# A kernel of two attentions and two expert mixtures: new written-out orders of all engines and new PSUM banks

## What is computed

```python
x = x + _L0_xattn_ref(_layernorm(x), ctx_768, Wq, Wk, Wv, Wo, bo)       # 8 heads of 64
x = x + _L0_ffn_ref(_layernorm(x), w_gate, w1_e, w3_e, w2_e, w1_s, w3_s, w2_s)
x = x + _L1_xattn_ref(_layernorm(x), ctx_768, Wq, Wk, Wv, Wo)           # 16 heads of 8
x = x + _L1_ffn_ref(_layernorm(x), router_w, experts_bias, w1, w3, w2, sw1, sw3, sw2)

# _L0_ffn_ref: 16 experts of 64, sigmoid scores, 2 of 4 groups, 4 experts
scores = jax.nn.sigmoid(x @ w_gate.T)
w = w / (w.sum(-1, keepdims=True) + 1e-06) * ROUTE_SCALE
routed = jnp.einsum('tef,ehf,te->th', silu(x w1_e) * (x w3_e), w2_e, combine)
return (routed + shared).reshape(shape)

# _L1_ffn_ref: 8 experts of 256, the 2 of the highest logits
logits = xf @ router_w.T + experts_bias
rw, sel = jax.lax.top_k(logits, K)
rw = jax.nn.softmax(rw)
moe_out = jnp.einsum('te,teh,ehd->td', cw, silu(g) * u, w2)
```

## Time and profile before

| | us |
|---|---|
| median of 3 runs | 230.97 |
| profiled execution, device time | 231.44 |
| its span | 229.6 |
| PE busy in the span | 223.2 |
| DVE busy | 164.1 |
| ACT busy | 152.8 |
| POOL busy | 126.4 |

### The profile page before, as it was taken

The page is one execution under the profiler, slowest core; times in us unless marked ns, Lnnn a source line. Parts: engine busy times, 40 slices in busy tenths (PEclk is TensorE's granted clock), DMA queues, the critical chain, the costliest instruction groups (busy, mean ns, idle before and its releaser), DMA issues.

```text
span 229.6 us, 4315 instructions
## 1 busy us (share of the span) xinstructions
PE 223.2 (97%) x1389; PEld 166.7 (73%) x1389; DVE 164.1 (71%) x482; ACT 152.8 (67%) x376; POOL 126.4 (55%) x127
## 2 busy tenths in 40 slices
PE   7999999999999999999999999999999999999994
PEld 3576765965889898889535563588878888888883
DVE  3689984788667963699948983564867785776874
ACT  2579999986679445672689778876464554645561
POOL 2866742899046927857492107208499500996540
PEclk9999999999999999999999999999999999999999
DMA  6790000000029925900600000027000003700002
GB/s 207 202 302 7 0 3 0 0 3 1 3 80 238 370 105 148 218 3 4 217 3 3 3 1 6 0 67 305 0 0 0 3 0 97 274 0 4 0 0 91
DMA packets 10172, 17.04 MB, mean 74 GB/s; under 512 B 3715, under 2 KB 5540, under 8 KB 9766
## 3 DMA queue, kind: packets, MB, share of 16 engines
q1 hardware_dynamic: 9926, 16.45, 23.0%
q10 hardware_dynamic: 224, 0.32, 0.4%
HBM read 16.08 MB, written 0.62 MB: 73 GB/s over the span
## 4 chain that ended last, share of the span: by engine, by line
PE 86%; ACT 6%; DVE 4%; POOL 2%; issue 1%; DVEq 0%; POOLq 0%
PE psum L1181 12%; PE psum L1185 11%; PE psum L1182 11%; PE psum L1354 7%; ACT prob L749 5%; PE psum L1416 5%; PE psum L1362 4%; PE psum L1364 3%; PE psum L1363 3%; PE psum L1472 3%; PE psum L1300 3%; PE psum L1312 3%; PE psum L1437 2%; PE psum L1276 2%; PE psum L1189 2%; PE psum L1460 2%
## 5 line engine op out<-in xcount | busy, mean ns | idle before, releaser
L703 POOL TENSOR_TENSOR act_s<-act_s,spread 128x512 f32<-128x512 f32 x35 | 44.3, 1289 | 20.2 <-DMA spread<-cw 14.1
L1181 PE MATMUL psum<-xT_hi,w_hi 128*128 128x512 f32 x108 | 43.9, 406 | 0.0
L1185 PE MATMUL psum<-xT_lo,w_hi 128*128 128x512 f32 x108 | 42.3, 391 | 0.0
L1182 PE MATMUL psum<-xT_hi,w_lo 128*128 128x512 f32 x108 | 42.1, 390 | 0.0
L798 ACT CAST q<-psum 128x512 fp32r<-128x512 f32 x35 | 20.4, 587 | 21.4 <-PE psum L1364 15.1
L1009 DVE TENSOR_TENSOR q<-psum,q 128x512 fp32r<-128x512 f32 x35 | 23.8, 687 | 13.5 <-ACT q L798 13.0
L788 ACT ACTIVATE act_s<-psum 128x512 f32<-128x512 f32 x39 | 23.1, 597 | 12.3 <-PE psum L1185 7.9
L1152 DVE TENSOR_REDUCE neg_max<-psum 128x2 f32<-128x308 f32 x64 | 26.2, 472 | 4.6 <-PE psum L1416 4.4
L703 POOL TENSOR_TENSOR hid<-hid,spread 128x512 f32<-128x512 f32 x13 | 16.5, 1286 | 18.7 <-DMA spread<-cw 14.4
L652 POOL TENSOR_TENSOR rstd<-vareps,minus_half 128x4 f32<-128x4 f32 x8 | 8.1, 1018 | 33.4 <-DVE vareps L910 33.4
L646 POOL TENSOR_TENSOR w_lo<-w_src,w_hi 128x768 fp32r<-128x768 f32 x12 | 21.8, 1835 | 8.6 <-ACT w_hi L718 8.6
(11 more groups left out here) (173 smaller groups left out, 467.0 us busy)
## 6 DMA issues: line engine op xcount, KB each, us to landing
spread<-cw SPq DMA_DIRECT2D x16, 256.0 KB, 4.6
spread<-cw SPq DMA_DIRECT2D x6, 512.0 KB, 5.6
w_src<-in_w SPq DMA_DIRECT2D x2, 1152.0 KB, 5.1
w_src<-in_w SPq DMA_DIRECT2D x1, 2304.0 KB, 10.9
spread<-cw SPq DMA_DIRECT2D x8, 128.0 KB, 2.9
w<-in_w SPq DMA_DIRECT2D x1, 576.0 KB, 6.6
out<-X SPq DMA_DIRECT2D x4, 128.0 KB, 1.8
wv<-in_wv SPq DMA_DIRECT2D x2, 192.0 KB, 4.8
```

The source lines that it names most:

```text
L703: pool.tensor_tensor(g, g, spread[:, slot, :], ALU.mult).then_inc(weighed, 1)
L1181: pe.matmul(dst, w_hi, xT_hi[:, b, :], start=True, stop=False)
L1182: pe.matmul(dst, w_lo, xT_hi[:, b, :], start=False, stop=False)
L1185: return pe.matmul(dst, w_hi, xT_lo[:, b, :], start=False, stop=True)
```

## The change

The table `PROGRAM` gets new strings for all five engines, and new banks for PE's steps. The steps are the same; what a step computes doesn't change. In the new order on PE, among others: the first xT goes ahead of three of the four kT; xT(1,0) goes ahead of the third k1 and of two pT steps; one scores step goes ahead of the first wo. On ACT, 21 `score` steps stand ahead of the fourth pT copy of batch 0, where there were 19; six `place_k1` go behind the first q1 copies of batch 0; three splits of `w2_1` go behind the last exponentials. On SP, `fetch w13_1` goes ahead of the fifth spread, and `fetch w2_1` one place_max later.

With the orders come waits that no longer lean on them. `need` (new) remembers for each engine and semaphore the highest count waited for and issues a wait only when it asks for more; `wait_filled` and `wait_moved` go through it. Waits that one step made for all that followed it on its engine are now asked by each step (`loaded`, `lo_of`, `xT_rounded`). DVE's `res` no longer waits for its own read; the lnA of sublayer 2 does.

```diff
@@ -150,68 +150,68 @@
 
 PROGRAM = {
     "PE":
-        "kT.0 kT.1 kT.0 kT.2 xT.3 vf.1 vf1.4 q.2 q.3 q.4 xT.2 q.3 scores.4.0 scores.3.1 scores.2.5 scores.6.7 " +
-        "scores.0.4 vf.3 q.1 q.2 scores.3.5 scores.6.1 vs.7 pT.2 scores.7.0 pT.4 q.3 pT.2 q.5 pT.6 scores.1.4 " +
-        "pT.7 pT.5 pT.2 k1.6 pT.0 scores.1.7 pT.2 pT.0 pT.5 pT.2 scores.6.4 rest.2.0.1.3 scores.7.5 pv pv pv " +
-        "pv scores.7.0 scores.1.2 scores.3.4 pT.6 wo.5 pT.0 pT.6 wo.1 scores.0.5 pT.3 pT.2 k1.4 vf1.6 vs1.0 " +
-        "pT.5 pT.3 pT.1 pT.2 k1.7 xT.6 k1.2 pT.4 pT.1 pT.6 gate.3 rest.1.6.4.5 pv pv pv pv h1.4 h1.6 wo.5 " +
-        "wo.1 cwT.3 h1.4 h1.3 h3.1 h3.4 h1.7 h3.1 xT.3 h3.0 h1.6 h3.5 gate.3 h3.7 h3.2 down.4 down down h1.1 " +
-        "h1.6 h1.0 h3.1 h3.5 h3.0 down h1.6 down down down down cwT.3 h3.1 down h1.0 h3.3 h1.4 h1.0 h3.5 h1.4 " +
-        "h1.6 xT.2 down.7 h3.4 h1.0 qd.2 down down q1.2.6.3.1 down score1.2 score1.5 h3.0 score1.2 score1.3 " +
-        "score1.6 score1.1 score1.5 h1.4 score1.3 score1.2 h1.6 down score1.5 score1.1 score1.3 score1.0 h3.4 " +
-        "score1.6 score1.1 score1.5 score1.2 down h3.4 h3.6 mT.5 down score1.5 score1.4 down score1.5 " +
-        "score1.4 score1.6 down expT.4.5 score1.6 score1.2 expT.1.0 expR.7 expR.3 score1.4 score1.5 score1.6 " +
-        "score1.2 expT.4.1 score1.5 xT.6 score1.2 score1.7 rest1.3.5 score1.0 qd.6 mT.0 expT.1.7 pv1 " +
...
+        "kT.7 xT.6 kT.5 kT.4 kT.3 q.2 q.4 q.6 q.5 xT.7 scores.2.6 vf1.3 scores.1.4 scores.0.5 scores.2.7 q.6 q.1 " +
+        "vf1.4 vs.3 scores.0.6 scores.5.1 scores.2.4 pT.7 pT.3 q.0 pT.7 q.6 scores.5.7 scores.3.1 pT.0 pT.2 k1.4 pT.6 " +
+        "vf.5 scores.7.0 scores.6.2 pT.3 pT.1 pT.5 pT.7 pT.4 pT.0 vf.5 rest.3.6.1.0 scores.7.4 pv pv pv pv scores.5.2 " +
+        "scores.6.1 scores.4.0 scores.7.3 wo.5 pT.2 pT.6 pT.1 wo.5 k1.0 pT.6 pT.2 vs1.7 pT.1 pT.4 xT.3 pT.6 pT.2 k1.0 " +
+        "h1.4 gate.3 pT.7 pT.0 pT.2 h3.6 rest.5.1.7.2 k1.0 pv pv pv pv wo.1 cwT.3 wo.2 h1.7 h1.5 h3.2 h3.4 h1.1 h1.3 " +
+        "h1.6 xT.7 down.5 h3.3 h1.1 h3.6 h3.2 gate.7 h1.4 down h1.3 down h3.1 down down down h1.3 h3.2 h3.1 down " +
+        "cwT.7 down down h1.7 h1.1 h1.2 h1.3 h1.6 h3.4 xT.1 h3.7 down.4 qd.2 h3.0 h1.7 down q1.5.3.1.6 down score1.2 " +
+        "h3.5 h3.3 score1.7 score1.0 score1.2 h1.5 h3.7 score1.0 score1.1 score1.5 score1.2 h3.3 score1.0 score1.1 " +
+        "down score1.6 score1.7 score1.2 h3.5 score1.3 down h1.6 score1.1 score1.0 score1.2 score1.3 score1.7 down " +
+        "h3.0 down mT.1 score1.6 score1.0 score1.5 score1.2 score1.1 down down expT.7.6 expR.1 expR.2 score1.4 " +
+        "score1.5 score1.0 score1.3 expT.7.1 score1.6 score1.2 score1.4 expT.5.7 score1.0 xT.3 rest1.6.1 mT.4 qd.0 " +
...
     "ACT":
-        "kT split lnB kT xT kT kT lnB q xT q split " + 16 * "score " +
-        "pT score score pT k1 pT score pT score score split score pv pv score pv pv place_k1 score score " +
-        "score score score split score score place_k1 pT score score place_k1 lnB pT k1 pT xT split k1 pT " +
-        "gate split k1 place_k1 place_k1 place_k1 pv pv pv pv place_k1 place_k1 h1 cwT h1 h1 h1 lnB place_k1 " +
-        "place_k1 xT place_k1 place_k1 h1 gate place_k1 h1 place_k1 h1 h1 h1 place_k1 place_k1 h1 cwT split " +
-        "split h1 h1 lnB h1 h1 xT h1 qd split h1 q1copy q1copy q1copy q1copy split h1 split split h1 mT exp " +
-        "exp exp expR lnB expR xT exp exp exp qd mT exp exp q1copy q1copy q1copy q1copy expR expR exp exp exp " +
-        "exp split split od exp exp mT exp exp split od expR exp exp exp onT expR mT exp exp exp exp exp expR " +
...
+        "lnB split xT kT kT kT lnB q kT xT q score score score score score score score score score score score pT " +
+        "score score score score score pT k1 score score score score pT score pT split split place_k1 score score pv " +
+        "score pv pv place_k1 pv score place_k1 score score score score pT score split score k1 place_k1 score lnB xT " +
+        "split pT pT k1 split pT gate k1 pv pv pv pv cwT h1 lnB h1 h1 h1 h1 h1 xT place_k1 place_k1 gate h1 h1 h1 " +
+        "place_k1 place_k1 h1 place_k1 cwT split h1 h1 split place_k1 lnB h1 xT h1 h1 qd q1copy h1 q1copy split split " +
+        "q1copy h1 q1copy split place_k1 place_k1 place_k1 place_k1 place_k1 place_k1 split h1 mT exp expR exp expR " +
+        "exp lnB exp xT exp exp mT qd exp exp q1copy q1copy q1copy q1copy exp exp expR expR exp exp od exp mT exp exp " +
+        "exp od expR expR exp exp onT exp exp mT exp exp exp exp lnB expR expR exp exp exp exp xT exp exp exp od " +
...
     "DVE":
-        "lnA sel lnA xT vf1 q q vf xT " + 9 * "score " +
-        "norm score vf q q score norm score vs score pT score score pT norm score q q pT norm score pT score " +
-        "pT pT score k1 pT score pT score score norm " + 8 * "score " +
-        "norm pT wo pT norm wo score lnA score pT norm pT vf1 pT k1 pT xT pT pT gate route route route route " +
-        "wo wo lnA k1 h3 vs1 xT k1 gate h3 " + 3 * "h3 route " +
...
+        "lnA xT lnA q q score score xT score score score score score vf1 norm q q score vf1 score score vs norm score " +
+        "pT score pT score q score norm score q score score pT norm pT score score vf score k1 score pT pT pT pT " +
+        "score vf norm score score sel norm score score score score score score score wo norm pT score pT wo lnA k1 " +
+        "norm pT pT pT xT vs1 k1 pT pT gate pT route route route route wo wo h3 lnA h3 xT h3 gate h3 route route h3 " +
...
     "Pool":
-        "lnA split lnA bo bo split " + 7 * "norm " + "lnA norm place_k1s split split split lnA place_k1s " +
-        8 * "weigh " + "split split lnA " + 8 * "weigh " +
-        "split split lnA split place_k1s place_k1s split split split lnA split split weigh weigh weigh weigh " +
-        "weigh lnA " + 27 * "weigh ",
+        "lnA split lnA norm norm norm norm bo norm split place_k1s norm split bo norm lnA norm split split lnA weigh " +
+        "place_k1s split weigh weigh weigh weigh weigh weigh weigh lnA weigh weigh weigh split weigh weigh weigh " +
+        "weigh split split place_k1s weigh lnA split place_k1s lnA split split split weigh weigh weigh weigh weigh " +
+        "weigh split weigh weigh lnA weigh weigh weigh weigh split weigh weigh weigh weigh weigh weigh weigh weigh " +
+        "weigh weigh weigh weigh weigh weigh weigh weigh weigh weigh weigh weigh ",
     "SP":
-        "store spread spread spread spread spread fetch store spread spread spread spread spread place_max " +
-        "fetch place_max place_max place_max store spread spread spread spread spread store spread spread " +
-        "spread spread spread out out out out ",
+        "store spread spread spread spread fetch spread store spread spread spread spread spread place_max place_max " +
+        "fetch place_max place_max store spread spread spread spread spread store spread spread spread spread spread " +
+        "out out out out ",
 }
 
 
@@ -434,10 +434,19 @@
...
+        reached = {}
+
+        def need(eng, semaphore, n):
+
+            at = (id(eng), id(semaphore))
+            if n > reached.get(at, 0):
+                eng.wait_ge(semaphore, n)
+                reached[at] = n
...
         def wait_filled(eng, key):
 
             k, n, _ = uses[key]
-            eng.wait_ge(bank_ready[k], n)
+            need(eng, bank_ready[k], n)
 
...
         def wait_moved(eng, key):
 
-            eng.wait_ge(*reads_of(key))
+            need(eng, *reads_of(key))
@@ -814,8 +823,7 @@
                     g, j = step[1:]
                     if j == 0:
                         wait_moved(act, ("k1", g))
-                        if g == 0:
-                            act.wait_ge(loaded["const"], 16 * N_CONST)
+                        need(act, loaded["const"], 16 * N_CONST)
                     k = k_stack[:, g % 2, :].bitcast(F32).rearrange("p (b c) -> p b c", b=B)
                     act.mul(k1[:, :, g, j, :], k[:, :, 0:CTX], head_rows[:, j:j + 1]).then_inc(k1_placed, 1)
@@ -897,6 +905,8 @@
                     s, b = step[1:]
                     if (s, b) == (0, 1):
                         dve.wait_ge(loaded["x1"], 16)
+                    if s == 2:
+                        wait_moved(dve, ("y", 1, b))
                     settle()
@@ -1000,7 +1010,6 @@
                     xb = X[:, b * T:(b + 1) * T, :]
                     settle()
                     moved(dve.tensor_tensor(xb, bank(key).rearrange("p (t d) -> p t d", t=T), xb, ALU.add), key)
-                    wait_moved(dve, key)
@@ -1173,15 +1182,12 @@
 
         @block.tensor
         def _(pe):
-            def product3(dst, w_hi, w_lo, s, b, first):
-
-
-                if first:
-                    pe.wait_ge(xT_rounded, position[("xT", s, b)])
+            def product3(dst, w_hi, w_lo, s, b):
+
+                need(pe, xT_rounded, position[("xT", s, b)])
                 pe.matmul(dst, w_hi, xT_hi[:, b, :], start=True, stop=False)
```

(14 more changed lines are left out.)

51 lines of the change are left out of this document (24 added, 27 removed), and 30 rows, old and new, of the table PROGRAM.

## The result

The changed kernel takes 239.46 us (median of 4 executions, 238.68 to 240.09) against 231.28 us for the kernel before beside it: a ratio of 1.034, 95% interval 1.029 to 1.040. It is 8.2 us slower, where 231.6 us and a range up to 234.0 were forecast. The profiled execution has a span of 238.3 us, 8.7 more than before.

A forecast was written before the change was run, and what follows sets the result against it. PE was taken as the bound, busy all but 3% of the span, with ACT setting the pace in the first attention. The terms 0 + 1.1 + 0.5 + 0.3 - 0.1 - 1.2 + 0 = +0.6 gave 231.6 us, range 228.8 to 234.0.

The forecast's parts named there:

- rival 4: Start: PE stands 0.8 us after one key product, clock halves until the first scores, 5.6 us more, 237; chance 0.02.
- First steps: Start: first layer norm's transposes ahead of three key products, earlier and later rows cancel; 0, 0.4 us either way.
- Term A: First attention: two more score steps ahead of the fourth pT copy delay rest, wo and xT(1,0); +1.1 us, ends 0, +2.0.
- the prediction's own sign (49.6): Sublayer 1's first transposes start near 50.3 us; a start at 49.6 or earlier would show term A wrong.
- Term B: First mixture, SP queue: fifth spread lands behind the fetch at 82.7 us, delaying batch 0's last down; +0.5, ends 0, +1.8.
- Layer norms: Sublayers 2 and 3: fewer products cover xT(2,0), +0.3 us; xT(2,1) -0.1; sublayer 3 covered, 0.
- Term C: Second attention: three splits leave ACT, 2.5 us less work, half given back; -1.2 us, ends 0 and -2.5.
- Second mixture: From the second mixture to the end: PE is the bound in both orders; 0, ends 0 and +0.4 us.
- `need`: Waits throughout the kernel: dropped or added waits occupy no engine; 0 us.
- rival 8: Second attention, from a later experiment moving w2_1 splits: PE waits for DVE's maxima, exponentials have room; 231.3, within 0.3 us.
- Rival 3: Second attention: score1 of the last head group waits for late place_k1 on ACT; 1 to 2 us more, about 233; chance 0.03.

The follow-up runs named there:

- a3_sp: The changed kernel with the fetch of w13_1 back behind the fifth spread on SP; 236.28 us, ratio 1.022.
- a1_fill: The changed kernel with two more warm-up products on PE between the first key product and the first xT; 237.75 us, ratio 1.029.
- b3_start: The kernel before with the changed kernel's waits and its first steps alone, on PE, ACT and DVE; 233.93 us, ratio 1.012.
- b2_fetch: The kernel before with one exchange on SP, the fetch of w13_1 ahead of the fifth spread of batch 0; 235.09 us, ratio 1.016.
- d1_lnb: a5_fills with one exchange on ACT, lnB(3,1) behind hsplit 7 and h1 11 of the second mixture; 235.56 us, ratio 1.018.
- b1_need: The kernel before's own orders and banks with the changed kernel's waits; 231.30 us, ratio 1.001.
- c3_mix: The kernel before with the changed kernel's orders and banks from xT(1,0) to the last down of sublayer 1, SP as before; 234.66 us, ratio 1.013.
- a5_fills: The changed kernel with SP's whole old order and filling products ahead of the first xT and of xT(2,1); 236.13 us, ratio 1.020.

## Why the prediction was wrong

**Of 8.2 us the sum had 0.6.** At full clock the changed kernel without the fetch's exchange takes 235.4 us, 4.1 more than before (a3_sp); that alone is above the range, so without the clock and the fetch the forecast would have failed too. At full clock with the exchange it takes 237.1 (a1_fill, 0.5 of its own products included): the exchange is worth 1.7 at most, and the falls of the clock 2.4 at least. The two profiled executions divide it more finely. The changed kernel is 2.4 us behind a3_sp at vs1 (49.50 and 47.13 us), where only the clock differs, 2.7 at the last down ahead of the late weighs (86.24 and 83.51), 4.8 at xT(2,0) (95.89 and 91.13), and 4.8 near the end. So there the clock took 2.4 and the late spread 2.0, and a3_sp itself is 3.8 behind the kernel before.

- **The clock (rival 4, chance 0.02) is the largest single part.** The mechanism and its place were named, the price of 5.6 us was too high (2.4 at vs1; the half rate ended at about 14.7 us, 0.83 being the mean of 14 to 16 us, and not at the first scores at 16.63), and the chance far too low. The step that failed was the argument that pauses of the same size stand in stretches at full clock. The pause was put at 0.8 us and was 2.21 (1.24 in a3_sp, where the key product began at 5.86 us as before; in this execution the warm-up was shorter, 3.90 us against 4.63, and it began at 5.17). The pauses from 115 to 141 us, to which I compared it, are small pieces. A second place, 118 to 124 us, was not seen at all; it lies in the very stretch that I took as safe. And the trace without a fall was one execution: of 46 executions of the kernel before that ran beside the experiments, four had a mean clock of 0.991 to 0.993 and took 232.3 to 232.8 us, where the 25 at 1.00 have a median of 231.0. The Trainium skill, "TensorE: Matmul & The Clock Gate", Part 1, has the throttled state as the default that activity releases; the falls to 0.50 behind pauses of 2.21, 2.40 and 1.83 us agree with it.
- **First steps, priced 0 with 0.4 either way.** Right in the changed kernel at full clock (the first `scores` at 14.25 us in a3_sp, 14.13 before), wrong by themselves (1.7, b3_start).
- **Term A, 1.1.** The size was right, the way to it only in part. In a3_sp, at full clock, `rest` starts at 33.04 us (32.38 before, 33.7 forecast), half of the delay forecast, and the delay is nearly gone at vs1. PE stands ahead of xT(1,0), as forecast, but xT starts at 49.64 us and not at 50.3, by the prediction's own sign (49.6) almost a refutation (timeline of PE):

```profile
49.64 0.73 PE L1243 MATMUL psum<-ident,xn 128*128 128x128 f32 x4 [1.02 <-ACT xn L731]
```

When both orders have done the same steps behind it (k1(3) comes next in the kernel before, at 50.01 us, h1(1,0,0) in a3_sp, at 51.17), the lag is 1.2 us, and still 0.9 at xT(1,1) of the kernel before (67.26 us, against 68.20 for h1(1,0,5)), when that has had its wait of 0.53. Nearly all of it is what PE takes for the pT and k1 steps that were put behind xT (1.1, forecast 1.2). The two score steps were forecast to delay xT by 0.7 and delay it by 0.1; that the total came out all the same is partly luck.
- **Term B, 0.5, ends 0 and 1.8.** The mechanism was right: POOL stands for a DMA ahead of its last two weighs. In the kernel before the landing came as forecast (82.88 us in b2_fetch against 82.7), but PE was there 2.40 us early: I had compared the landing with the last down, and the down before it needs the first late weigh already. In the changed kernel at full clock the size was nearly right too. The two downs in a3_sp, and then in a1_fill with the exchange (timelines of PE):

```profile
83.51 1.05 PE L1354 MATMUL psum<-w,hid 128*128 128x128 f32 x8
...
84.65 2.05 PE L1354 MATMUL psum<-w,hid 128*128 128x128 f32 x16
```

```profile
83.98 1.05 PE L1357 MATMUL psum<-w,hid 128*128 128x128 f32 x8
...
85.64 2.39 PE L1357 MATMUL psum<-w,hid 128*128 128x128 f32 x16 [0.50 <-DVE hid L1124]
```

From the first of these downs to xT(2,0) a3_sp takes 7.62 us, a1_fill 8.49: the exchange costs 0.9 us there, and 2.0 in the changed kernel's own profile. The step that failed is that the landing was left at 82.7 us while PE's road was moved back: in that profile the late two landed at 86.97, 3.5 later than in a1_fill (83.52), where PE was only 2.3 later (86.24 and 83.98). 2.3 of the 3.5 are the later issue of the spreads (68.03 and 65.77 us), and the fetch itself took 12.6 us instead of 10.7; why is open. "Served in the order of issue" held: the longest of the spreads took 12.5 us from issue to landing in the changed kernel, 11.7 in b2_fetch and 11.3 in a1_fill, against 6.4 in the kernel before. The trace agrees with the rule that was cited from the Trainium skill, "DMA: Bandwidth & Descriptors", section "Queues, rings and completion order".
- **Layer norms, 0.2.** From the lag of 1.2 us above to the first pv1 of the second attention a3_sp lost another 1.4 us (2.6 behind), though it has neither the fetch nor a fall in it. The step that failed was counting products between a producer and its transpose and taking the rest at PE's pace. For xT(2,0) the count was right: PE stood 0.34 us for its rows, 0.3 forecast. For xT(2,1) it stood 0.44. (The two rows of rows 6 are y(1,1) and xT(2,1); xT(2,0) started at 90.52 us.) But PE's idle time in the whole stretch is only 1.4 us against 1.1 in the kernel before; the other 1.1 stand in the trace as busy time of the same products at full clock, in pieces that no wait names.
- **Term C, -1.2.** The sign of the stretch was right, the size not: 0.6 in the changed kernel, 0.1 from the splits alone. Idle time taken off ACT did not come back. PE's listed waits there in the kernel before were 0.5 us for DVE's maxima and 0.2 for ACT, which fits rival 8 but doesn't prove it.
- **Second mixture, 0 with an end of 0.4.** Measured 1.7. "PE is the bound in both" was read from stretches from 180 us on. In a3_sp 0.7 arise from wo1 to h1(3,0,7) (157.61 us in the kernel before), 1.0 from there to 197 us, and nothing behind; of the 1.0 some 0.6 lie behind one lnB that waits with two ready steps behind it (d1_lnb).
- **`need`, 0:** right (b1_need). Rival 3 (`place_k1`) didn't come.

What stays open: how the 1.4 us between xT(1,0) and the second attention divide among the steps, since the borders of c3_mix have a price of their own, and why one execution of b3_start took 235.5 at a clock of 0.998. Nothing tried was faster than the kernel before.

## What to carry to other kernels

When a step of the busiest engine is moved ahead, ask how long that engine then stands with nothing queued, and price the rate behind the pause too: the pauses of 2.40 and 2.21 us cost up to 1.6 and 2.4 us more by it. A late transfer is to be compared with the first step that needs it, not the last, and its landing moves with the steps that feed it. One order's slack is not another's: a stage in which an engine is busy throughout says nothing of how many tenths a new order loses at its borders. Put steps that are ready ahead of one that waits for a layer norm.

## What the runs showed of the hardware

The granted clock fell behind single pauses of about 2 us (1.83, 2.21, 2.40), and didn't fall behind the pauses of 1.24 us in a3_sp and 1.67 in the changed kernel. In a stretch of many small pauses it fell in some executions of the same kernel only (a1_fill: two of four, 1.9 us between the two pairs; the trace of one shows it from 118 to 124 us), and with products put into the pauses in none of nine (a5_fills, d1_lnb). Where it fell, products took twice as long: 4.63 against 2.40 us for the same twenty records. One kernel thus has two times, a3_sp 235.4 and 237.2, that no order explains; the kernel before has them too, in four of 46 executions.
